# A third V job ahead of the first score, and the second norm and late weight loads in other slots

## The reference

```python
def reference(x, w_qkv, b_qkv, w_out, b_out, gate_w, up_w, down_w, gate_s, up_s, down_s):
    xn = _layernorm(x)
    q, k, v = split(xn @ w_qkv.T + b_qkv)               # 16 heads of 32
    scores = q @ k.T / sqrt(32), masked to the lower triangle
    a = softmax(scores) @ v
    attn = a @ w_out.T + b_out
    g = (xn @ gate_w.T) * gate_s
    u = (xn @ up_w.T) * up_s
    ffn = ((silu(g) * u) @ down_w.T) * down_s
    return x + attn + ffn
```

## Time and profile before

| | us |
|---|---|
| timed executions | 1915.85, 1929.38, 1929.62 |
| their median | 1929.38 |
| the profiled execution | 1921.82 |
| its span, first to last instruction | 1918.6 |
| TensorE busy | 1857.7 |
| VectorE busy | 1504.7 |
| ScalarE busy | 1441.9 |
| GpSimd busy | 1262.0 |

### The profile page before, as it was taken

One profiled execution on the slowest core, in us unless ns is written; L12 is line 12 of the kernel. 1 busy time (PEld: TensorE's weight loads), 2 busy tenths in 40 slices (PEclk: granted clock), 3 DMA queues, 4 the chain that ended last, 5 costly groups with the idle time before them and its releaser, 6 DMA issues.

```text
span 1918.6 us, 44219 instructions
## 1 busy us (share of the span) xinstructions
PE 1857.7 (97%) x14978; PEld 1220.3 (64%) x14978; DVE 1504.7 (78%) x4516; ACT 1441.9 (75%) x4263; POOL 1262.0 (66%) x1799
## 2 busy tenths in 40 slices
PE   6899999999999999999999999999999999999997
PEld 4566666666656666566666756666566666766664
DVE  5777778787787877878777787887878778787786
ACT  4786777868778777787877778677777877778775
POOL 5765857758577676766857576575765767566463
PEclk9999999999999999999999999999999999999999
DMA  9978969789697897978879797886978869797785
GB/s 227 163 158 158 184 133 198 147 157 182 129 200 146 168 163 140 188 136 180 165 142 194 138 178 144 157 167 125 199 128 160 160 133 186 128 186 137 125 162 110
DMA packets 818551, 305.93 MB, mean 159 GB/s; under 512 B 756176, under 2 KB 793168, under 8 KB 818320
## 3 DMA queue, kind: packets, MB, share of 16 engines
q1 hardware_dynamic: 796176, 240.79, 70.0%
q0 software_dynamic: 22144, 62.27, 12.9%
HBM read 55.59 MB, written 16.78 MB: 38 GB/s over the span
## 4 chain that ended last, share of the span: by engine, by line
PE 72%; DVE 11%; ACT 5%; POOL 5%; DMA 3%; issue 3%; SPq 1%; ACTq 0%; DVEq 0%; POOLq 0%
PE bank L256 72%; DVE phl L571 3%; ACT phl L471 3%; DVE bank L561 2%; DMA pt<-phl 2%; DVE res L598 1%; ACT bank L479 1%; DVE small L536 1%; POOL ht L784 1%; DVE xhl L713 1%; DVE fh L586 1%; POOL qkp L757 1%; DVE ft L581 1%; POOL ht L782 0%; POOL att L767 0%
## 5 line engine op out<-in xcount | busy, mean ns | idle before, releaser
L479 ACT ACTIVATE bank<-bank,small 128x512 f32<-128x512 f32 (+3 forms) x1024 | 516.8, 506 | 205.6 <-DVE small L561 205.1
L571 DVE SCALAR_TENSOR_TENSOR phl<-bank,small,phl 128x512 f16<-128x512 f32 (+3 forms) x1024 | 526.5, 545 | 156.5 <-ACT phl L471 153.4
L561 DVE CUSTOM_DVE_ANT_0 bank<-bank,mask 128x512 f32<-128x512 f32 (+3 forms) x1024 | 484.0, 504 | 165.6 <-PE bank L256 163.1
L471 ACT ACTIVATE phl<-bank,small 128x512 f16<-128x512 f32 (+3 forms) x1024 | 501.0, 532 | 44.7 <-DMA pt<-phl 34.3
L256 PE MATMUL bank<-xnT,wg 128*128 128x256 f16 x2816 | 367.1, 273 | 4.5 <-DVE fh L586 4.5
L256 PE MATMUL bank<-xnT,wu 128*128 128x256 f16 x2816 | 366.4, 273 | 0.0
L256 PE MATMUL bank<-xnT,wqkv 128*128 128x512 f16 x1536 | 352.2, 379 | 1.6 <-DVE q L605 1.6
L256 PE MATMUL bank<-wd,ht 128*128 128x512 f16 x1408 | 314.3, 379 | 4.4 <-POOL ht L784 4.2
L256 PEld LDWEIGHTS bank<-xnT,wg 128*128 128x128 f16 x2816 | 263.6, 98 | 66.1 <-DVE fh L586 5.3
L256 PEld LDWEIGHTS bank<-xnT,wu 128*128 128x128 f16 x2816 | 276.3, 98 | 32.6
L256 PE MATMUL bank<-stk 96*128 96x512 f16 (+3 forms) x1024 | 245.4, 300 | 16.0 <-DVE phl L571 12.7
(11 more groups left out here) (97 smaller groups left out, 2192.2 us busy)
## 6 DMA issues: line engine op xcount, KB each, us to landing
stk<-qkp SPq DMA_DIRECT2D x768, 64.0 KB, 2.2
res<-in_x_dram POOLq DMA_DIRECT2D x64, 256.0 KB, 4.9
xin<-in_x_dram POOLq DMA_DIRECT2D x60, 256.0 KB, 3.8
out_dram<-res POOLq DMA_DIRECT2D x60, 256.0 KB, 4.1
pt<-phl SPq DMA_TRANSPOSE x512, 4.3
xin<-in_gate_dram POOLq DMA_DIRECT2D x11, 256.0 KB, 3.8
xin<-in_up_dram POOLq DMA_DIRECT2D x11, 256.0 KB, 3.7
xin<-in_down_dram POOLq DMA_DIRECT2D x11, 256.0 KB, 3.8
```

The source lines that it names most:

```text
L471: i = eng.activation(part(qt, j)[:, j % 2, 0], pb[:, off:off + W], ACT.Copy, scale=st_r[:, c:c + 1])
L479: i = eng.activation(pb[:, off:off + W], pb[:, off:off + W], ACT.Exp, bias=st_m[:, c:c + 1], scale=-1.0, accum_out=st_s[:, c:c + 1])
L561: i = eng.tensor_tensor_reduce(out=bk[:, off:off + W], in0=bk[:, off:off + W], in1=mask[:, 512 - W:512], scale=-(32.0 ** -0.5) / (QS * QS) ...
L571: i = eng.scalar_tensor_tensor(part(qt, j)[:, j % 2, 1], pb[:, off:off + W], st_r[:, c:c + 1], part(qt, j)[:, j % 2, 0], ALU.mult, ALU.sub ...
```

## The change

Five edits, all of order. The third V job, (0, 1, 0), which stood in slot 0 behind the first score, stands ahead of slot 0, and the fourth moves from slot 1 to slot 0. The tiles of batch 1's norm are in slots 3, 6, 10 and 13 in place of 3, 7, 11 and 15. The three loads of down weights are in slots 4, 7 and 9 in place of 1, 3 and 5. The loads of `dsc` and `bout` stand behind the stacking of group 0 in SyncE's queue, in place of ahead of the last four weight chunks. The scaling of `dsc` on GpSimd is in slot 9 in place of the prologue.

```diff
@@ tables and the order of jobs
         if b == 0:
-            v_at[0] = (0, 1, 0)
-            v_at[1] = (0, 1, 1)
+            v_at[0] = (0, 1, 1)
...
-            norm_at[40 * b - 40 + 4 * t + (3 if b == 1 else 0)] = (b, t)
+            norm_at[40 * b - 40 + ((3, 6, 10, 13)[t] if b == 1 else 4 * t)] = (b, t)
...
+    job(("v", 0, 1, 0), v_vl, 3)
...
-    ffn_load_at = {1: (12,), 3: (13,), 5: (14,)}
+    ffn_load_at = {4: (12,), 7: (13,), 9: (14,)}
@@ TensorE; ScalarE has v_high(0, 1, 0) and VectorE v_low(0, 1, 0) in the same place
         for f in range(F_FIRST):
             gate_up(f)
+        v(0, 1, 0)
         for n in range(LAST):
@@ GpSimd
-        w.wait_ge(d_small[3], 16)
-        eng.tensor_scalar(dsc[:, :], dsc[:, :], 1.0 / HS, 1.0, op0=ALU.mult, op1=ALU.mult).then_inc(p_set, 1)
         load_xin(xin_load_at[-1])
...
+            if n == 9:
+                w.wait_ge(d_small[3], 16)
+                eng.tensor_scalar(dsc[:, :], dsc[:, :], 1.0 / HS, 1.0, op0=ALU.mult, op1=ALU.mult).then_inc(p_set, 1)
@@ SyncE
-        for i, (dst, src) in enumerate(((dsc, down_s), (bout, b_out))):
-            eng.dma_start(dst[:, :], src.to_broadcast([128, 512])).then_inc(d_small[i + 3], 16)
         for n in range(8, NCH):
             load_weight(n)
         stack(0, 0, (0, 1, 2))
         stack(0, 1, (0, 1, 2))
+        for i, (dst, src) in enumerate(((dsc, down_s), (bout, b_out))):
+            eng.dma_start(dst[:, :], src.to_broadcast([128, 512])).then_inc(d_small[i + 3], 16)
```

More of the change, by code:

```diff
@@ L502, in scalar_program @@
             tanh(f)
+        v_high(0, 1, 0)
         for n in range(LAST):
@@ L688, in vector_program @@
             hidden(f)
+        v_low(0, 1, 0)
         for n in range(LAST):
```

## The result

The changed kernel takes 1933.84 us in the median (19 executions, 1927.63 to 1942.85), the kernel before 1926.23 us (19 executions, 1915.85 to 1940.18). The ratio is 1.004 with a 95% interval of 1.0024 to 1.0055: slower by 7.6 us, clear of noise and inside 1%. A second comparison gave 1.0036 (1.0015 to 1.0058). The profiled execution took 1927.63 us, the fastest of its 19, with a span of 1924.2.

The account below looks back on a forecast made before the run. TensorE, 97% busy, was taken as the bound, so only its idle time and low clock before about 110 us could yield. Terms summed to -3.8 us, set against a 1925.6 median: about 1922 us, range 1908 to 1932.

Parts of the forecast that it names:

- rival C: VectorE's statistics in slots 10 and 13: norm tiles arrive behind the down weights, about 1928 to 1934 us; chance 0.13.
- a difference that lies behind 230 us, where I expect none: Sign that would show the forecast wrong: any time difference after the first 230 us of the run, none being expected.
- The purse: TensorE before about 110 us: 12.0 us idle plus at most 3.2 of low clock, 15.2 us or 0.8% to gain.
- The down weights, -1.1: Slots 4, 7, 9: fewer loads beside the probabilities' transposes, shortening ScalarE's 2.23 us wait at 64.47; 1.1 us gained, ends 2.2 and 0.
- The V job, -2.6: In TensorE's 3.25 us hole ahead of the first score: everything behind comes 2.62 us nearer; ends 3.25 gained and 0.
- rival B: Lead swallowed at TensorE's 2.85 us wait, as VectorE frees the bank no earlier; 1.5 gained to 1 lost, about 1925; chance 0.23.
- The row vectors, -0.3: Two loads fewer ahead of the last four weight chunks: the rest of the first-score hole shrinks, 0.3 us gained, ends 0.63 and 0.
- The norm, -0.5 + 1.0 + 0.5: Slots 3 to 13: earlier statistics gain 0.5 us; third tile's wait costs 1.0, its transpose ahead of the probabilities' 0.5.
- Low clock, -0.8: TensorE between 70 and 110 us: shorter waits bring back some of 3.2 us lost to low clock, 0.8 us gained.

Follow-up runs that it names:

- tiles ahead of the down weights: Kernel before with down weights' loads in slots 4, 8, 9 and, in slots 4 and 8, the norm tile's load issued first: 1.0036 (1.0019 to 1.0053).
- down weights undone: Changed kernel with the down weights' loads back in slots 1, 3, 5, all else as changed; against the kernel before: 1.0016 (1.0000 to 1.0032).
- down weights earlier: Kernel before with the down weights' loads in slots 0, 1, 2 in place of 1, 3, 5: 1.0017 (0.9998 to 1.0036).

## Why the prediction failed

The sign was wrong. I took 1922 as likeliest and 1932 as the upper end, and gave "slower" 0.13 as rival C, whose own times reached 1934. Of the 7.6 us, 5.4 to 6.0 by the marks lie where I wrote "a difference that lies behind 230 us, where I expect none". The rest is inside the interval (4.6 to 10.6 us).

**The purse** bounded what the edit could gain and was no bound on a loss: I looked at idle time up to 230 us, and the edit made idle time near 910 and 1830 us.

**The down weights, -1.1.** This is the term that failed: alone they measured +0.44%, some 8 us. Locally it came out at about nothing. The wait I had set out to remove went, and waits for two tiles (1.92 and 1.10), a gate block (3.98) and the first product's transposes (3.02) came; by the fifth product no lateness can be told. With the down weights alone the transpose issued at 52.8 took 8.3 us where it took 11.2, but the one issued at 63.1 took 8.8 where one issued at 64.2 took 4.4, and the tiles took 7.0 and 8.1 us for 5.7 and 4.4: the crowding moved and didn't shrink. That is the 0 which the prediction drew for this term from the Trainium skill, page "DMA: Bandwidth & Descriptors", section "Issuing engines are not separate DMA queues" (DMAs issued by any engine run on the same 16 engines and interleave); these landing times agree. One reading was off too: the 9.25 us in the chain are of the transpose issued at 55.13, not of the one at 52.7 that took 11.2. The step missing from my working is that a DMA moved within GpSimd's queue shifts that queue's own stops. I had its rows before me: the 1.61 us at 899.96 and the bracket at 1819.93 are in the trace of before.

**The V job, -2.6.** The hole, its length and the first score were as forecast. The step that failed is "I take nearly the whole": alone it measured 1.0003, 0.6 us more in place of 2.6 less, with an interval from 2.9 less to 4.0 more, which only just lets the 2.6 in. My rival B had the lead swallowed at the 2.85 us wait by VectorE's work; in the kernel after it was swallowed earlier, at 47.85, by a DMA. The first tile's statistics were not among my moved rows, as their slot is the same. But VectorE was ready for them at 47.85 - 3.12 = 44.73, 2.5 us earlier than before, and their load landed at 47.8 where it had landed at 46.7. Before, it had half a microsecond in hand. With the V job alone that wait was nothing and 0.82 us; there the wait ahead of the gate block, rival B's place, grew from 2.85 and 2.86 us to 3.50 and 3.32, and half of the lead (1.3 us in the means of two traces each) was left behind it. Where the other half went is not shown.

**The row vectors, -0.3.** The sign is doubtful. I looked at what they leave (the weight chunks) and not at what they go to: issued at 36.1 and 36.8, they share the DMA engines with the first tile, whose landing went from 8.3 to 10.9 us. With the V job this measured 1.0049, and without it 1.0014, within noise. The traces are worse than that: with the row vectors there and the down weights still in slots 1, 3 and 5, the down loads took 12.4 to 16.1 us to land (8.2 to 10.8 before), and the first transpose of probabilities 18.7 and 19.6 (7.7 before). The three kernels of this kind have their sixth product at 232.64, 234.08 and 236.56, against 227.50 and 232.03 in the kernel before, one trace each.

**The norm, -0.5 + 1.0 + 0.5.** The third tile did wait, 2.11 and 2.74 us, within the ends of 0 to 3.5. The wait behind the transposes went from 2.73 to 6.28 in the first trace of the changed kernel but was 2.32 in the second, so no growth is shown; with the tiles' transposes put back, the time stayed. By itself the norm is no more than 0.4%, and nothing in the company of the others.

**Low clock, -0.8.** It went the other way. The mean granted clock was 0.9936 with the down weights alone (12 executions) and 0.9958 in the kernel before on that chip (31), with mean spans of 1930.0 and 1920.9. Taking (1 - clock) x span as an estimate of what the low clock costs, it is 12.4 against 8.1 us, so that 4.3 of the 9.1 us are clock and the rest is idle time.

**Rival C** had the right side, and the wrong mechanism: tiles ahead of the down weights gave 1.0036 with no wait for a tile, and the same stops at 906 and 1826 us as in the changed kernel.

**Open.** What GpSimd waits for at these DMAs isn't in the profile. The stops are 98 DMAs apart (130 and 228, 131 and 229, 132 and 230), which points to something that is counted along that queue; no run measured what. It isn't a plain count from the start: these kernels issue the same DMAs ahead of number 130, only numbers 14 to 18 in another order, and the trace has the same number of GpSimd's instructions ahead of it. Two ratios don't fit the two late places: V job with row vectors, 1.0049, and the down weights in slots 42 to 46, 1.0061, both without them; one trace of each (sixth products at 232.64 and 232.92) is not enough to say where those lose. Nor do the parts add up: down weights alone 1.0044 and V job with row vectors 1.0049, but all together 1.004. Rests of 1683 us in two traces without the two late places (down weights undone, down weights earlier) are the wait near 1605 us. And no run took the stop away with the down weights in their new slots, which would have been the last proof.

## What to carry to other kernels

A loss can lie far from the edit: put marks along the whole run and compare several traces before explaining the waits nearest to it, since two traces of the kernel before differ by 5.5 us at the second attention product, and two of the changed kernel by 8.0 us from the sixth product to the last. When a DMA is moved in GpSimd's queue, look in the trace for that queue's stops ("issue" ahead of a DMA row, and DMAs issued long after their data) and ask which transfer the stop will fall on. When work is moved forward into a hole, list every DMA awaited behind it; the lead beyond the smallest slack among them is lost there.

## What the hardware showed that I had not expected

GpSimd stood still 1.6 to 4.6 us at single DMA issues with nothing to wait for in the profile, with lengths that repeat to 0.01 us between executions, 98 DMAs apart, and the places move by one DMA when the three down loads change theirs more than 100 DMAs earlier.

A wait can be paid twice on TensorE: behind 3.4 to 4 us idle, the next block of twelve matmuls took 4.44 us for 2.75, and one of 22 took 6.60 for 4.91, some 1.7 us each; behind 3.41 us idle twelve took 3.98. Length alone doesn't tell: 3.02 us ahead of the first attention product were followed by 3.39 us for 1.81, but 2.85 us ahead of a gate block by one of 1.05, and 2.44 us by one of 1.56. At the late place 2.22 us ahead of a score were followed by 22 down matmuls in 6.61 us in the first trace of the down weights alone, and in 4.92 with the tiles ahead of the down weights.
